# Second layer's decay differences: from TensorE products of spread gates to ScalarE subtractions on running sums loaded into all partitions

## The reference

```python
q, k, v = (conv_silu(xn @ W.T) for W in (Wq, Wk, Wv))      # 6 heads of 64; q and k are l2-normalized
g = -exp(A_log) * softplus(xn @ Wa.T + dt_bias)            # log decay, per token and head
def step(S, inputs):
    S = S * exp(g_t); kv = k_t @ S; u = b_t * (v_t - kv)
    S = S + outer(k_t, u); return S, (q_t * scale) @ S
x = x + s * silu(relu(xn @ sign(up).T * up_scale) @ sign(down).T * down_scale * output_scale)
```

## Time and profile before

| what | us |
|---|---|
| median of 3 runs (1363.28 to 1366.1) | 1363.5 |
| the profiled execution's own time | 1364.62 |
| its span, first to last instruction | 1361.7 |
| PE busy in the span | 1315.0 |
| DVE, ACT, POOL busy | 1063.5, 737.4, 528.7 |

### The profile page before, as it was taken

The page is one execution under the profiler, slowest core; times in us unless marked ns, Lnnn a source line. Parts: engine busy times, 40 slices in busy tenths (PEclk is TensorE's granted clock), DMA queues, the critical chain, the costliest instruction groups (busy, mean ns, idle before and its releaser), DMA issues. The chain is left out here.

```text
span 1361.7 us, 24113 instructions
## 1 busy us (share of the span) xinstructions
PE 1315.0 (97%) x8866; PEld 640.7 (47%) x8866; DVE 1063.5 (78%) x1855; ACT 737.4 (54%) x1307; POOL 528.7 (39%) x434
## 2 busy tenths in 40 slices
PE   5888999999999999999999999999999999999998
PEld 2333333333333333333344546855486555855475
DVE  7888978778877887788884985778776976868846
ACT  5675666556655666556657552455334652355431
POOL 3499953012211221112222763247431762328431
PEclk9998999999999999999999999999999999999999
DMA  6520000010000000000254024002311024001121
GB/s 232 190 81 8 7 9 3 15 41 14 9 17 32 24 7 7 24 30 15 87 196 184 20 52 82 25 24 60 51 44 40 8 71 82 17 32 43 34 46 47
DMA packets 80468, 68.50 MB, mean 50 GB/s; under 512 B 46080, under 2 KB 67296, under 8 KB 77792
## 3 DMA queue, kind: packets, MB, share of 16 engines
q1 hardware_dynamic: 67936, 65.39, 15.5%
q10 hardware_dynamic: 12416, 1.57, 1.1%
HBM read 44.87 MB, written 17.87 MB: 46 GB/s over the span
## 5 line engine op out<-in xcount | busy, mean ns | idle before, releaser
L621 DVE TENSOR_REDUCE mS<-vpair 128x1 f16<-128x512 f32 x512 | 329.1, 685 | 111.6 <-PE vpair L1125 109.5
L936 ACT ACTIVATE probs<-bank 128x512 f16<-128x512 f32 x512 | 277.1, 594 | 163.0 <-PE bank L1132 162.8
L1179 PE MATMUL bank<-rows,both 128*128 128x512 f16 x1024 | 243.0, 380 | 0.4 <-DVE th L650 0.3
L436 POOL TENSOR_TENSOR h<-th,h 128x512 f16<-128x512 f32 x61 | 71.4, 1171 | 213.2 <-ACT h L907 213.2
L1179 PEld LDWEIGHTS bank<-rows,both 128*128 128x128 f16 x1024 | 91.3, 98 | 121.2 <-issue 13.9
L2257 PE MATMUL bank<-rows,both 128*128 128x512 f16 x512 | 118.6, 382 | 0.0
L1125 PE MATMUL vpair<-qk 32*128 32x512 f16 x512 | 100.3, 387 | 13.1 <-DVE mS L621 7.7
L2273 PE MATMUL bank<-both,hid 128*128 128x512 f16 x512 | 111.2, 379 | 0.0
L2241 PE MATMUL bank<-rows,both 128*128 128x512 f16 (+1 forms) x456 | 104.0, 379 | 0.9 <-PEq L160 0.9
L1132 PE MATMUL bank<-qv,qk 32*128 32x512 f16 x512 | 99.7, 386 | 0.0
L1193 PE MATMUL bank<-dn,h 128*128 128x512 f16 x256 | 98.0, 383 | 0.0
(11 more groups left out here) (363 smaller groups left out, 2654.1 us busy)
## 6 DMA issues: line engine op xcount, KB each, us to landing
h<-in_ug SPq DMA_DIRECT2D x8, 1024.0 KB, 5.5
lt_scratch<-big SPq DMA_DIRECT2D x16, 384.0 KB, 2.7
dn<-in_down SPq DMA_DIRECT2D x2, 2048.0 KB, 11.1
x_scratch<-th SPq DMA_DIRECT2D x16, 256.0 KB, 2.2
res<-x_scratch SPq DMA_DIRECT2D x16, 256.0 KB, 4.3
out_x<-res SPq DMA_DIRECT2D x16, 256.0 KB, 2.0
both<-in_w SPq DMA_DIRECT2D x2, 1548.0 KB, 10.4
t_scratch<-tok SPq DMA_DIRECT2D x16, 192.0 KB, 2.1
```

The lines of the kernel that those rows point to most:

```text
L436: pool.tensor_tensor(h16(ft, 1), row32, h16(ft, 0), ALU.subtract).then_inc(S["row_lo"], 1)
L621: v.tensor_reduce(mS[:, u % 2, qt, 32 * j + DH:32 * j + DH + 1], SA[n % 2][:, :], AX.X, ALU.max).then_inc(S["max_done"], 1)
L936: a.activation(probs[:, n % (2 * G), :], SB[n % 2][:, :], ACT.Exp, scale=float(DH) ** -0.5).then_inc(S["p_ready"], 1)
L1179: mm = pe.matmul(GB[n % 2][:, :], w[:, kt, col:col + P], xnb(b, kt), start=r == 0, stop=r == 2 * KT - 1)
```

## The change

The decay from i to j is exp(c[j] - c[i]) with the running sums c of g within the tile. Now PE makes the sums twice: down the partitions (in "vec", as before) and, by one more fp32 product of 128 columns, as rows (24 rows, one per tile and head). ACT copies the rows to sT and the columns to gsum. SP stores sT (12 KB) to DRAM, waits for that, and loads each tile's six rows into all 128 partitions of gU (128 x 768 fp32, 384 KB a tile). ACT's `fall(tt, hf)` makes Relu(c[i] - c[j]) on gU in place, one instruction per head (bias is a column of gsum), three per call; `decays(tt)` is one Exp of 128 x 768. `spread` and `differences` are gone. The masks stay at their places in POOL's list, but each waits for the whole `decays(tt)`. One semaphore of layer 0 (t_mh) is merged into another (t_m), at the same places.

```diff
-        a += [(b, "pre", m) for m in range(1, 5)] + [(b, "vec"), (b, "DT", 0, 0), (b, "DT", 0, 1), (b, "pre", 5)]
-        a += [(b, "DT", 1, 0), (b, "DT", 1, 1), (b, "pre", 6), (b, "pre", 7), (b, "pre", 8)]
-        a += [(b, "DT", 2, 0), (b, "DT", 2, 1), (b, "sT"), (b, "DT", 3, 0), (b, "DT", 3, 1)]
+        a += [(b, "pre", m) for m in range(1, 5)] + [(b, "vec")] + [(b, "pre", m) for m in range(5, NM)] + [(b, "sT")]
...
+                def load_sums(tt):
+                    if tt > 1:
+                        sp.wait_ge(S["dec_r"], b * DECAYS + 2 + (tt - 1) * (LH + 1))
+                    sp.dma_start(gU[tt % 2].rearrange("p h c -> p (h c)"), bass.AP(s_dram.tensor, (TT * LH + tt * LH) * P, [[0, P], [1, LH * P]])).then_inc(S[f"gs_in{tt % 2}"], 16)
...
+                sp.wait_ge(S["dec_r"], b * DECAYS + 1)
+                sp.dma_start(s_dram[1], sT[:, :]).then_inc(S["gs_out"], 16)
+                sp.wait_ge(S["gs_out"], (b + 1) * 16)
+                for tt in range(3):
+                    load_sums(tt)
                 store_matrices(0)
+                load_sums(3)
...
-                def spread(tt):
...
-                    pool.tensor_tensor(gU[tt % 2], over(upto, LH), hb(gg[:, tt, :], P), ALU.mult).then_inc(S["gU_r"], 1)
...
                 def mask(tt):
                     for hf in range(2):
-                        pool.wait_ge(S["a_took"], AI[b, "DT", tt, hf] + 1)
+                        pool.wait_ge(S["dec_r"], b * DECAYS + 2 + (tt + 1) * (LH + 1))
...
+                def fall(tt, hf):
+
+                    a.wait_ge(S[f"gs_in{tt % 2}"], (b * 2 + tt // 2 + 1) * 16)
+                    for hh in range(hf * HH, hf * HH + HH):
+                        a.activation(gU[tt % 2][:, hh, :], gU[tt % 2][:, hh, :], ACT.Relu, scale=-1.0,
+                                     bias=gsum[:, tt * LH + hh:tt * LH + hh + 1]).then_inc(S["dec_r"], 1)
 
                 def decays(tt):
...
+                    if tt > 1:
+                        a.wait_ge(S["v_took"], VI[b, "KQ", tt - 2, 1] + 1)
+                    a.wait_ge(S["dec_r"], b * DECAYS + 2 + tt * (LH + 1) + LH)
+                    a.activation(GT[tt % 2], gU[tt % 2], ACT.Exp, scale=-1.0).then_inc(S["dec_r"], 1)
...
+                bk = take("vec")
+                a.activation(sT[:, :], bk[0:TT * LH, SUM_COL:SUM_COL + P], ACT.Copy).then_inc(S["dec_r"], 1)
+                a.activation(gsum[:, :], bk[:, 0:TT * LH], ACT.Copy).then_inc(S["dec_r"], 1)
...
+                mm = pe.matmul(bk[0:TT * LH, SUM_COL:SUM_COL + P], gg.rearrange("p t h -> p (t h)"), upto, start=True, stop=True)
```

More of the change, by code:

```diff
@@ L480, in _ @@
                     pool.tensor_tensor(W["rs"], W["rs0"], W["expo"][:, 0:TT], ALU.pow).then_inc(S["t_rs"], 1)
-                    pool.wait_ge(S["t_m"], 2)
+                    pool.wait_ge(S["t_m"], 4)
                     pool.partition_all_reduce(W["ama"], W["am"][:, 0:2], P, bass.bass_isa.ReduceOp.max).then_inc(S["t_m"], 1)
@@ L720, in weight_max @@
                 v.tensor_reduce(W["am"][:, 2 * i:2 * i + 1], W["wst"][:, 2 * i:2 * i + 2], AX.XY, ALU.max,
-                                apply_absolute_value=True).then_inc(S["t_mh"], 1)
+                                apply_absolute_value=True).then_inc(S["t_m"], 1)
             def weight_maxima():
                 am = W["am"]
-                v.wait_ge(S["t_mh"], 2)
+                v.wait_ge(S["t_m"], 2)
                 v.tensor_tensor(am[:, 0:1], am[:, 0:1], am[:, 2:3], ALU.max).then_inc(S["t_m"], 1)
@@ L730, in weight_scales @@
                 ama, pw, ipw = W["ama"], W["pw"], W["ipw"]
-                v.wait_ge(S["t_m"], 3)
+                v.wait_ge(S["t_m"], 5)
                 v.tensor_scalar(ama, ama, 1e-30, None, ALU.max).then_inc(S["pow_a"], 1)
@@ L1292 @@
 WO_COL = 3 * TT * LH
+SUM_COL = P
+DECAYS = 2 + TT * (LH + 1)
 def bank_order():
@@ L1365, in layer1 @@
         vec = sb("vec", [P, TT, 3 * LH])
+        gsum = sb("gsum", [P, TT * LH])
         gcs = sb("gcs", [P, TT, MT])
@@ L1440, in layer1 @@
             "pe": ["v_full", "a_full", "f_full", "down_full", "sq_used", "kv_full"],
-            "act": ["a_took", "RT_r", "tanh_c", "tb_r", "ez_r", "lz_r", "tap", "gate_t", "osq", "th_r", "r32_r", "inv_a", "yh_r"],
+            "act": ["a_took", "RT_r", "tanh_c", "tb_r", "ez_r", "lz_r", "tap", "gate_t", "osq", "th_r", "r32_r", "inv_a", "yh_r", "dec_r"],
             "dve": ["v_took", "kv_took", "st_r", "mv_r", "rs0_r", "xs_r", "xh_r", "xl_r", "conv", "sil_r", "beta_r", "az_r",
@@ L1444, in layer1 @@
                     "out_r", "snm_r", "ls_r", "sub", "wo_r"],
-            "pool": ["rs_r", "sq_r", "rn_r", "gU_r", "GTm_r", "eye_r", "T0_r", "orn_r", "gw_r", "hid_r", "zeros"],
-            "sp": ["xb_in", "res_in0", "res_in1", "out0", "out1", "s_out", "s_in", "lt_out", "lt_in",
+            "pool": ["rs_r", "sq_r", "rn_r", "GTm_r", "eye_r", "T0_r", "orn_r", "gw_r", "hid_r", "zeros"],
+            "sp": ["xb_in", "res_in0", "res_in1", "out0", "out1", "s_out", "s_in", "gs_out", "gs_in0", "gs_in1", "lt_out", "lt_in",
                    "t_out", "t_in0", "t_in1"],
@@ L2092, in _ @@
                 evict_pre(1)
-                def three_mats(dst, fn, *key):
-                    a.activation(dst[:, key[-1]:LH:2, :], take(*key)[:, 0:HH * P].rearrange("p (h c) -> p h c", h=HH), fn).then_inc(S["a_took"], 1)
+                def fall(tt, hf):
[3 more added lines that the diff above has]
+                                     bias=gsum[:, tt * LH + hh:tt * LH + hh + 1]).then_inc(S["dec_r"], 1)
                 def decays(tt):
[L2097 to L2101, removed]
+                    if tt > 1:
+                        a.wait_ge(S["v_took"], VI[b, "KQ", tt - 2, 1] + 1)
+                    a.wait_ge(S["dec_r"], b * DECAYS + 2 + tt * (LH + 1) + LH)
+                    a.activation(GT[tt % 2], gU[tt % 2], ACT.Exp, scale=-1.0).then_inc(S["dec_r"], 1)
                 tanh_conv(0)
@@ L2124, in _ @@
                 evict_pre(5)
-                decays(1)
                 tanh_conv(4)
+                a.wait_ge(S["dec_r"], b * DECAYS + 2)
+                fall(0, 0)
                 evict_pre(6)
+                fall(0, 1)
                 if b == 0:
@@ L2132, in _ @@
                 hidden(2)
+                past(a, "T0_r", b * TT * 2)
+                decays(0)
                 evict_pre(7)
+                fall(1, 0)
                 tanh_conv(6)
                 hidden(3)
+                fall(1, 1)
                 evict_pre(8)
+                decays(1)
+                fall(2, 0)
+                fall(2, 1)
                 decays(2)
                 hidden(4)
+                a.wait_ge(S["gs_out"], (b + 1) * 16)
                 a.activation(sT[:, :], take("sT")[0:TT * LH, 0:P], ACT.Copy).then_inc(S["a_took"], 1)
+                fall(3, 0)
+                fall(3, 1)
                 decays(3)
@@ L2383, in cols @@
                     return slice(HD * hh, HD * hh + HD)
[L2385 to L2389, removed]
                 up_tile(1)
-                differences(0)
                 pre_tile(5)
                 squares(2)
-                differences(1)
                 pre_tile(6)
@@ L2406, in _ @@
                 pairs("KQ", 0, 0)
-                differences(2)
                 pairs("KK", 1, MT)
@@ L2411, in _ @@
                 pe.transpose(bk[0:TT * LH, 0:P], sn.rearrange("p t h -> p (t h)"), ident).then_inc(S["a_full"], 1)
-                differences(3)
                 pairs("KQ", 1, 0)
@@ L2634 @@
     lt = nc.dram_tensor("lt_scratch", (TT, LH, P + 1, P), F32, kind="Internal").ap()
-    sc = nc.dram_tensor("s_scratch", (TT * LH, P), F32, kind="Internal").ap()
+    sc = nc.dram_tensor("s_scratch", (2, TT * LH, P), F32, kind="Internal").ap()
     ti = nc.dram_tensor("t_scratch", (2, TT, SYS, BS, BS), F32, kind="Internal").ap()
```

15 lines of the change are left out of this document (3 added, 12 removed).

## The result

| | us |
|---|---|
| before, median of 4 runs (1363.28 to 1366.1) | 1363.5 |
| after, median of 4 runs (1413.81 to 1418.41) | 1415.8 |
| ratio after to before, 95% interval | 1.0377, 1.0363 to 1.0392 |
| forecast, its range | 1396.5, 1382 to 1410 |

The change makes the kernel 3.8% slower. The forecast had the sign and the place of the loss, and was 19 us short; the time lies outside its range. The profiled execution of the changed kernel took 1413.8 us, its span 1412.0, 50.3 more than the span before.

What follows compares the result with a forecast made beforehand. PE, busy in 97% of the span, was taken as the bound. Batches 1 to 3 at 6.7 us each plus 4.8 of clock, and batch 0's 8.2, add 33.1 to 1364.6: 1397.7, as median 1396.5; range 1382 to 1410.

Steps and rivals of the forecast that it cites:

- The load: SP's broadcast loads into gU: issued from about 912.2, landing in 3.8 us, upper end 5.5.
- ACT's steps: Added work on ACT: 0.9 us for a call of three falls, 0.85 for an Exp of 768 columns.
- The chain ahead of squares(5): evict_pre(8), Exp of decays(1), mask(1), hidden(2), square(5) in a row: PE idle 6.8 us, squares(5) 8.2 later.
- The new row product: One fp32 product of 128 columns added on PE: 0.23 us a batch.
- The merged semaphore: In layer 0, order of the steps unchanged: costs nothing.
- squares(4): PE waits 4.0 us for POOL's square(4) behind mask(0), starting 1.5 us later than before; bounds +0.1 to +3.3.
- The clock: Half clock behind the 6.8 us wait, 1.6 us in each of three batches, 4.8; batch 0 had paid already.
- Rival 3: Both waits pay the clock, or broadcast loads land at the upper end: about 1403; both with slow masks 1414; 20%.
- Behind squares(5): Two removed differences calls save 2.8 us, but KQ 1's bank waits for DVE: 1.5 us a batch gained.
- the three signs: Wrong if PE does not wait there, the wait is for a load, or the stage behind squares(5) stretches.
- the bank wait: KQ 1's bank needs DVE to have taken KK 1's first half; 1.4 to 1.5 gained, not 2.8.
- the gain stays: Rival: the squares do not wait, 16 us gained, 1347; 3%.

Runs made afterwards that it cites:

- run with fillers: Changed kernel plus unread PE products in the waits ahead of squares(4) (10, in batch 0 26) and squares(5) (28): 1397.1 us, ratio 1.0230 to before.
- reordered kernel: Changed kernel with square(4), square(5) ahead of POOL's masks, up tiles earlier on PE, ACT's hidden and DVE's conv and silu steps reordered: 1355.6 us, ratio 0.9930.
- both squares first: Changed kernel with square(4) ahead of mask(0), and square(5) ahead of mask(1) and hidden(2), in POOL's list: 1363.1 us, ratio 0.9979 to before.

## Why the prediction was wrong in size

**Right.** The load: issued at 924.19, the first fall at 928.30, a median of 3.8 us to landing as taken. ACT's steps: three falls in 0.97 us, the Exp 0.84 (0.9 and 0.85 predicted). The chain ahead of squares(5): a wait of 6.46 us against 6.8. The new row product took 0.33 us (920.59 to 920.92) against 0.23, a small miss. All of this was worked out from rows of other shapes, and held. The merged semaphore cost nothing that shows, as forecast: the first "vec" came at 747.2 us after, 748.5 before.

**squares(4): "after a wait of 4.0 us, and 1.5 us later than before".** Measured from the start of "vec", it came 1.0 us later (17.4 against 16.4), after a wait of 2.5. The masks and the square ran uncontended (1.95 and 1.04, where 2.1 and 1.4 were taken), and PE was not 2.5 us earlier at the place but 1.6, in part because squares(3) waited too (0.48). A small error, by which the kernel lost less than forecast there. (In batch 0 the wait was 5.8 us, and squares(4) came 3.8 later, where 3.1 had been put.)

**The clock: "A wait of 6.8 us with nothing in it should bring that in every batch; batch 0 has paid it already. So 3 x 1.6 = 4.8". This is the step that failed.** The run with fillers puts the half clock of the changed kernel at 20 us. Some 1.6 of it batch 0 had paid before, so some 18.4 were added where 4.8 had been put. The term was mis-sized in three ways. The first wait pays too (up_tile(3) 3.51 us instead of 1.89): 1.7 us in each of batches 1 to 3. What stands behind the second is a row of pieces that all run slow: the squares 1.87 instead of 1.05, KK 0 1.66 instead of 0.94, the up tile 3.60 instead of 1.90, then most of KQ 0. Against the kernel with fillers that is 3.6 us in batch 1, 2.4 in batch 2 and 3.7 in batch 3, in place of 1.6. And batch 0, with its waits of 5.8 and 6.5 us, pays as much as the others (3.3 and 1.9), not what it had paid before. The prediction kept as a rival that both waits pay, by a rule of the Trainium skill ("TensorE: Matmul & The Clock Gate", "The HAM clock gate": the low rate is the default, and sustained work releases it). The trace agrees in that the clock is at 0.50 behind both waits and rises while PE works. Rival 3 gave that 20% but priced it with the same 1.6 us, and so ended at 1403.

**Behind squares(5): "I take 1.5".** From squares(5) to `down_part` it took 32.1 us before and 35.7 after, +3.7 where -1.5 and +1.6 of clock had been put. That stage stretched instead of shrinking, one of the three signs that the prediction had named of being wrong. With the clock kept up by fillers it takes 32.1, as before, so nothing is left of the 1.5. The 2.8 us of removed products did go, but PE waited 0.81, 0.56 and 1.10 for DVE, 2.5 us a batch, which takes back all but 0.3. The first two waits, 1.4 together, are the bank wait that the prediction worked out (2.8 - 1.5 = 1.3). The third, at KQ 3, was not looked for. DVE's conv(8) stands between its passes KK 3 and KQ 2, and it took longer, beside three of POOL's hidden with hardly a pause between them, than before (2.75 us, beside two that stood apart):

```profile
968.90 3.98 DVE L1699 SCALAR_TENSOR_TENSOR res<-pre,both,res 128x512 f32<-128x512 f32 x3
```

**The sum, by its terms.** Forecast 33.1, measured 52 by the medians, 19 short: 18.4 - 4.8 = 13.6 of clock, 4 x 1.5 = 6 behind squares(5), and small errors of both signs at the squares that come to less than 1 together.

**The side with no loss.** The rival "the gain stays" (1347) had its condition named rightly, squares that do not wait, but put the gain of that case at 16 us; with that condition nearly made true, 3 us were gained (ratio 0.9979). What the prediction left out is that the pairs would then wait for DVE, 11 us in all, with half clock behind some of it, and that the up tiles, once moved to fill that wait, would wait for ACT (9.6 us).

**Open.** Why the clock falls behind a wait of 1.4 or 1.7 us in one batch and not in the next was not settled. No run took the contention of POOL with DVE away as a whole, so how much of the 3 us left above the work in the stage (51.4 of the reordered kernel against 53.6 - 5.3 = 48.3) belongs to it is not known.

## What to carry to other kernels

When a producer is moved to another engine and comes later, read the in-order list of every engine that consumes it, and ask what else is queued behind the consumer: here two squares of 1 us that did not need the new data, queued behind what did, cost 54 us. Price a wait of PE as its length plus what the half clock adds to all work behind it until the rows show the clock back, not to one group alone. And a product taken off a full PE is worth its time only once the lists of DVE, ACT and POOL are moved up as well; the waits for the next engine showed up one after the other, each only when the one before it was gone.

## What the runs showed of the hardware that was not expected

- The granted clock fell behind waits of PE of 0.89 us (before), 1.36 us (batch 0 of the reordered kernel) and 1.70 us (both squares first, batch 1: 0.50 from 935 to 940). It did not fall behind waits of 1.36 and 1.77 us in batch 0 and of 1.71 in batch 3 of that last execution. Eight idle products in the place of the wait ahead of KK 1 kept it at 1.00 in batches 1 to 3.
- In the changed kernel the clock stayed at 0.50 although PE was busy in every microsecond from 951 to 957, with squares, pairs and an up tile.
- Beside one of POOL's operations, DVE operations on 24 columns took 0.85 to 1.07 us instead of 0.18 to 0.24, whether it was POOL's mask or its hidden.
- A load that reads one 3 KB row into all 128 partitions (384 KB) landed in 3.8 us in the median, between the 2.9 of a plain store of that size and the 5.5 of a plain load of 1024 KB.
